# The first state products of a gated recurrence, made for one column instead of 512 and fed in as the gates' bias

## The reference, cut to what matters

```python
x = x + tanh(g_xattn[0]) * _L0_xattn_ref(_layernorm(x), ctx, ctx, ...)
x = x + tanh(g_ffn[0])   * _L0_ffn_ref(_layernorm(x), w_gate, w_up, w_down)
x = x + tanh(g_xattn[1]) * _L1_xattn_ref(_layernorm(x), ctx, ctx, ...)
x = x + tanh(g_ffn[1])   * _L1_ffn_ref(_layernorm(x), wf, uf, bf, ...)

# _L1_ffn_ref
c0 = jnp.broadcast_to(in_c, (batch, in_c.shape[0]))      # batch is 512 here
def step(c, xt):
    ft = sigmoid(xt @ wf.T + c @ uf.T + bf)
    it = sigmoid(xt @ wi.T + c @ ui.T + bi)
    gt = tanh(xt @ wc.T + c @ uc.T + bc)
    return ft * c + it * gt, None
c_final, _ = lax.scan(step, c0, x)                        # 4 steps
h = tanh(einsum('tbi,oi->tbo', x, wo) + c_final @ uo.T + bo)
```

## Time and profile before

| what | value |
|---|---|
| median of 3 runs | 343.23 us (343.20 to 343.27) |
| span of the profiled execution, first to last instruction | 341.2 us |
| what lies around the span (median less span) | 2.0 us |
| mean granted TensorE clock | 0.957 |
| PE busy | 279.0 us (82%) |
| DVE busy | 252.5 us (74%) |
| ACT busy | 192.6 us (56%) |
| POOL busy | 136.7 us (40%) |

### The profile page before, as it was taken

How to read it: one execution, slowest core, us unless ns; L and a number is a source line. 1 busy time by engine, 2 the same in 40 slices (tenths; PEclk the granted TensorE clock), 3 DMA queues, 4 the chain that set the end, 5 groups by cost and what they waited for, 6 DMA issues and landing times. The chain is left out here.

```text
span 341.2 us, 4468 instructions
## 1 busy us (share of the span) xinstructions
PE 279.0 (82%) x1424; PEld 160.7 (47%) x1424; DVE 252.5 (74%) x538; ACT 192.6 (56%) x303; POOL 136.7 (40%) x274
## 2 busy tenths in 40 slices
PE   0889899899989779985007888899998998999994
PEld 0558544455434345331005776664654654444462
DVE  5699875877996388889989977986596693441834
ACT  1673367556476746779589632446656446665232
POOL 6669893750050411870002059921386207131100
PEclk9999999999999999997556999999999999999998
DMA  7930100010000000000000002220001000000004
GB/s 204 336 146 3 69 32 10 27 73 10 1 8 3 0 0 2 1 0 0 1 0 0 2 0 92 94 100 2 10 25 76 8 0 10 1 0 3 0 1 123
DMA packets 9687, 12.55 MB, mean 37 GB/s; under 512 B 896, under 2 KB 5376, under 8 KB 9664
## 3 DMA queue, kind: packets, MB, share of 16 engines
q1 hardware_dynamic: 9232, 11.80, 9.7%
q10 hardware_dynamic: 432, 0.47, 0.7%
HBM read 4.27 MB, written 1.05 MB: 16 GB/s over the span
## 5 line engine op out<-in xcount | busy, mean ns | idle before, releaser
L1333 DVE TENSOR_REDUCE sb_nm<-ps_top 128x3 f32<-128x462 f32 (+2 forms) x168 | 96.0, 626 | 26.6 <-PE ps_top L953 13.9
L772 ACT ACTIVATE sb_pr<-ps_score 128x512 f32<-128x512 f32 (+1 forms) x148 | 82.3, 583 | 58.8 <-PE ps_score L985 49.2
L953 PE MATMUL ps_top<-sb_Kd,sb_Q 128*128 128x462 f32 (+3 forms) x240 | 69.7, 349 | 4.7 <-DVE sb_nm L1333 2.4
L985 PE MATMUL ps_score<-sb_Q,sb_Kd 128*128 128x512 f32 x119 | 54.4, 467 | 1.3 <-ACT sb_pr L772 1.0
L953 PEld LDWEIGHTS ps_top<-sb_Kd,sb_Q 128*128 128x128 f32 x240 | 42.6, 188 | 18.1 <-DVE sb_nm L1333 11.9
L626 POOL TENSOR_SCALAR sb_var<-sb_mv 128x4 f32<-128x4 f32 x16 | 4.7, 291 | 83.3 <-DVE sb_mv L1296 82.9
L985 PEld LDWEIGHTS ps_score<-sb_Q,sb_Kd 128*128 128x128 f32 x119 | 22.2, 188 | 31.6 <-ACT sb_pr L772 23.4
L1017 PE MATMUL ps_pv<-sb_pr,sb_V 128*32 128x512 f32 x256 | 34.1, 605 | 0.0
L620 POOL TENSOR_SCALAR_AFFINE_SELECT sb_pr<-sb_pr 128x512 f32<-128x512 f32 x16 | 10.6, 661 | 46.4 <-ACT sb_pr L772 46.4
L1353 DVE STREAM_TRANSPOSE sb_oq<-ps_pv 128x512 f32<-128x512 f32 x16 | 10.8, 700 | 12.4 <-PE ps_pv L1017 12.3
L643 POOL TENSOR_SCALAR sb_xn<-sb_xr,sb_nmean,sb_rstd 128x128 f32<-128x128 f32 x44 | 19.3, 453 | 1.2
(11 more groups left out here) (180 smaller groups left out, 556.5 us busy)
## 6 DMA issues: line engine op xcount, KB each, us to landing
sb_Q<-sb_qh SPq DMA_DIRECT2D x16, 256.0 KB, 2.3
sb_Q<-sb_ql SPq DMA_DIRECT2D x8, 256.0 KB, 3.3
sb_xr<-x SPq DMA_DIRECT2D x4, 256.0 KB, 7.7
out<-sb_xr SPq DMA_DIRECT2D x4, 256.0 KB, 2.5
sb_wsb<-w SPq DMA_DIRECT2D x1, 704.0 KB, 9.0
sb_wf<-wffn SPq DMA_DIRECT2D x1, 576.0 KB, 8.6
sb_wkr<-wkr SPq DMA_DIRECT2D x2, 256.0 KB, 7.1
sb_Q<-sb_nmT SPq DMA_DIRECT2D x16, 32.0 KB
```

Source lines behind the costliest of these rows:

```text
L772: act.activation(pr[:, k % PRING, q0:T], score_bank(B * layer + b, t)[:, q0:T], ACT.Exp, scale=SCALE).then_inc(exp_r, 1)
L953: ins = pe.matmul(cols[:, c0:c1, :], Q4[n % 3][:, g, P * qt:P * qt + P], Kd[n % 3][:, g, j:j + c1 - c0, 0:keys], start=True, stop=not mask ...
L985: ins = pe.matmul(ps[:, :], Kd[n % 3][:, g, j, 0:P], Q4[n % 3][:, g, :], start=True, stop=True, skip_group_check=True)
L1333: dve.tensor_reduce(nm[:, :, :].rearrange("p t h -> p (t h)")[:, f0:f0 + heads], top[k % MRING][:, 0:keys * heads].rearrange("p (h k) -> p ...
```

## The change

The initial state is equal in all columns, so its product with a recurrent weight is one column. The three state products of step 0 leave PE's slots 4, 6 and 8 of stage 3. In their place PE makes three products of one column each in the quantised block (`first_states`, into three columns of bank `top[1]`), DVE adds the gates' biases to them into a new tile `fcols` of 128 x 3 (`first_gates`, two instructions, ahead of the four `outer`), and ACT's first three gates take their bias from `fcols`. The input products of step 0 now start their PSUM banks themselves. Three waits on the new semaphore `fcol_r` and one on `fmul` come with it.

```diff
-           (4, "state0", "first"), (4, "step0", "first"), (6, "state1", "first"), (6, "step1", "first"),
-           (8, "state2", "first"), (8, "step2", "first"),
+           (4, "step0", "first"), (6, "step1", "first"), (8, "step2", "first"),
...
+        fcols = sb("fcols", [P, 3])
...
                 if b > 0:
                     act.wait_ge(c_r, b + 2)
-                bias = (hcols[:, BF:BF + 1], hcols[:, BI:BI + 1], cols_sb[:, BC:BC + 1])[k]
+                else:
+                    act.wait_ge(fcol_r, 2)
+                bias = ((hcols[:, BF:BF + 1], hcols[:, BI:BI + 1], cols_sb[:, BC:BC + 1])[k] if b > 0
+                        else fcols[:, k:k + 1])
...
+                if n == B and u == 0:
+                    pe.wait_ge(fcol_r, 2)
...
                     pe.wait_ge(c_r, b + 2)
-                    pe.wait_ge(top_red, units_before(2 * B))
-                if b > 0:
-                    pe.wait_ge(gt_r, 3 * b - 2 + k)
+                pe.wait_ge(gt_r, 3 * b - 2 + k)
...
+                if (b, k) == (0, 0):
+                    pe.wait_ge(top_red, units_before(2 * B))
...
-                ins = pe.matmul(top[k][:, :], weight((WF, WI, WC)[k]), pnT[:, b, :], start=(b == X_FIRST),
+                ins = pe.matmul(top[k][:, :], weight((WF, WI, WC)[k]), pnT[:, b, :], start=(b in (0, X_FIRST)),
...
+            def first_states():
+
+                pe.wait_ge(fev, 24)
+                pe.wait_ge(c_r, 2)
+                for k in range(3):
+                    ins = pe.matmul(top[1][:, k:k + 1], weight((UF, UI, UC)[k]), cst[:, 0:1], start=True, stop=True,
+                                    skip_group_check=True)
+                ins.then_inc(fmul, 1)
...
                     for k in range(2, 4):
                         global_top(k)
+                    first_states()
                     pe.wait_ge(fev, 24)
                     pe.wait_ge(o_r, 2)
                     keep_warm(6)
...
+                def first_gates():
+                    dve.wait_ge(fmul, 1)
+                    for k, bias in ((slice(0, 2), hcols[:, BF:BF + 2]), (slice(2, 3), cols_sb[:, BC:BC + 1])):
+                        dve.scalar_tensor_tensor(out=fcols[:, k], in0=top[1][:, k], scalar=1.0 if k.start else 0.5, in1=bias,
+                                                 op0=ALU.mult, op1=ALU.add).then_inc(fcol_r, 1)
...
                 factor(1, 1.0, sc[:, 3, 1:2], sc[:, 2, 1:2])
+                first_gates()
                 for c in range(B):
                     outer(c)
```

More of the change, by code:

```diff
@@ L369, in program @@
         gt_r, ct_r, c_r = sem("gt_r"), sem("ct_r"), sem("c_r")
+        fmul, fcol_r = sem("fmul"), sem("fcol_r")
         ymm, y_r = sem("ymm"), sem("y_r")
```

## The result

| | before | the change |
|---|---|---|
| median | 343.25 us (343.20 to 343.60, 4 runs) | 340.65 us (340.55 to 340.79, 4 runs) |
| span of the profiled execution | 341.2 us | 338.6 us |
| ratio | | 0.9925, 95% interval 0.991 to 0.994 |

The change is 2.6 us faster, 0.75%; the forecast was 340.75 in a range of 340.4 to 341.6.

The account below looks back on a forecast made before the run. The prediction took PE's queue in stage 3 of layer 1 as the bound: -2.58 us for the removed products plus 0.10 for the DVE pair gave -2.48, so 343.23 became 340.75 us, range 340.4 to 341.6.

Parts of the forecast that it names:

- PE's queue is the bound where the products stand, each worth 0.86: Stage 3 of layer 1: PE runs without waits, so removing three products of 0.86 us saves 2.58 us.
- The next bound doesn't eat it: Stage 3: ACT, score banks and DVE meet their waits after the removal, so the full 2.58 us remains.
- Behind tile 9 everything moves along: From exponential 9 on, ACT has no backlog; the bank exchange begins 2.58 us earlier and is as long as before.
- The rival in which the mask on POOL holds things up: ACT or POOL's mask holds the bank exchange, losing one product's worth: -1.72 + 0.10, so 341.6 us; chance 0.12.
- The columns end by 176.5 and cost nothing: Quantised block: three one-column products are ready by 176.5, while PE idles until 181.05, so they cost nothing on PE.
- The pair costs +0.10: Quantised block: DVE's two `first_gates` instructions ahead of `outer(0)` cost +0.10 us, between hidden and +0.48.
- The estimate worked out from the Trainium skill: Quantised block: at 120 cycles plus columns the DVE pair takes 0.25 us, is over at 177.32 and costs nothing.
- the 0.19 in front of `outer`: Quantised block: `outer(0)` begins 0.19 us after ACT's end; if set-up needing a free DVE, the pair costs +0.22.
- The clock: Rival: less busy PE drops to the lower clock, costing 7.9 us from 306.3 to 314.2, so 348.7 us; chance 0.02.

Follow-up runs that it names:

- five pairs: The change with the pair of DVE instructions made five times, each into its own three columns: 341.13 us, ratio 0.9940.
- the last three runs: On one chip: the change unedited, 341.01 us; without its one-column products and DVE pair, 341.04 us; with step 0's third input product in PE slot 11, 340.28 us.
- one product back, the first: The change with step 0's first state product made over 512 columns again, in slot 4: 341.52 us, ratio 0.9951.
- only the tile: The kernel before with nothing but the unused 3-column tile `fcols` added: 343.12 us, ratio 1.0001.
- columns where PE is full: The change with one more one-column product ahead of each of step 0's three input products: 341.60 us, ratio 0.9956.
- the third product back: The change with step 0's third state product made over 512 columns again, in slot 8: 341.31 us, ratio 0.9938.

## Why the prediction was right

- *PE's queue is the bound where the products stand, each worth 0.86.* Right, and shown: putting the third or the first back makes tile 9 later by 0.86 either way.
- *The next bound doesn't eat it.* Right for ACT and the banks: tile 9 moved by 2.58 against tile 4 (6.02 now, 301.17 - 292.57 = 8.60 before). DVE did become the later one at the new state, with 2.3 us of slack where I had reckoned 2.0.
- *Behind tile 9 everything moves along.* This step missed 0.16. I had taken it that the third mask on POOL moves along with the rest and stays as long. DVE's chain in front of the new state moved by 1.72 plus what `renew` allowed, so it no longer stands to the mask as before, and the two overlapped for 0.57 instead of 0.30. The run in which DVE waits for the mask gives the 0.16 back. The rival in which the mask on POOL holds things up was there, but priced at a whole product, 0.86.
- *The columns end by 176.5 and cost nothing.* Right; 1.28 us busy in place of the 1.8 reckoned, done at 175.48.
- *The pair costs +0.10.* Mis-sized, since it is 0.00 within 0.04. I had 0.34 for an instruction, from one of 128 columns and two partitions, and it is 0.16. The estimate worked out from the Trainium skill ("VectorE: DVE Perf Modes", section on the TRN2 errata), over by 177.32, came nearer: 0.22 from the first start to the last end, against 0.25. That is partly luck, since each of the two takes more than the estimate's 0.13 (0.16 and 0.15) and they overlap, where the estimate put one behind the other. And the 0.19 in front of `outer` isn't set-up of a free DVE, as the five pairs show.
- *The clock.* 1.00 in the stage, as before. What was taken away left PE as full as before, only for a shorter time. That no pause of PE brings the clock down is true of the stretch from 200 to 208 only: in the quantised block, where PE had waited 6.9 us for work, the granted clock was 0.50 in both kernels.

The two misses, 0.16 of loss not seen and 0.10 of cost that wasn't there, nearly cancel: the sum should have been 2.42 by the trace. That 340.75 came so near is in part luck. The medians differ by 2.60, and by 2.58 on the chip of the last three runs, but with intervals of 0.5 us to either side they can't tell 2.42 from 2.60.

The spans of the two traces differ by 2.60 as well. Behind step 1 they agree (341.2 - 306.45 = 34.75 before, 338.6 - 303.81 = 34.79 now), so some 0.2 lies ahead of tile 4. The changed instructions didn't bring it: at 173.40, before the first of them starts (174.20), the trace is already 0.24 ahead (DVE's reduction in front of the fourth maximum, 173.64 before), and from ACT's tiles to tile 4 both take 116.9. So does every other variant with a usable trace (116.8 to 116.9), but for the five pairs. What differs between executions is when ACT's tiles start: from 175.47 to 177.10 over twelve traces, 175.47 and 176.18 for the change itself. The four latest, 176.31 and up, are those in which PE's granted clock was 0.83 to 0.88 from 40 to 50 us (one product back, the first; five pairs; only the tile; columns where PE is full); the eight others had 1.00 there. What spreads those eight, and with it the 0.24, is not shown.

## What to carry to other kernels

An operand that is the same in every column can be multiplied once, where the engine idles, and come back as a bias that an instruction reads anyway; its worth is the full price of the products only where the chain runs through them without a wait. Slide the queue forward by what is removed and test each wait with its margin, and test the pairs of engines too that only hold each other up. A stretch that the busy rows show nearly full may be an exchange of two banks with room in it: the pitch of queued pieces tells, not the busy time, and moving a piece into such room is worth while only as long as what it feeds isn't late.

## What the runs showed of the hardware

The same POOL instruction, an affine select over 128 x 512 in f32, takes 0.64 us alone and 0.80 or 1.06 beside DVE's f32 instructions with two SBUF operands: 0.64 when DVE waited for it, 0.80 with an overlap of 0.30 us (303.76 against DVE's last instruction until 304.06), and 1.06 with 0.57. So it does not run slower for a share of the overlap: it loses all of it but 0.14 to 0.15. Put otherwise, it ends 0.49 to 0.50 behind the end of DVE's instruction, however long the two overlap (302.02 against 301.53 in the change, 304.56 against 304.06 before, 302.74 against 302.24 with the third product back), as if it stood still until DVE was done. DVE's instruction, which had begun first, kept its 0.69. Where DVE waited for the mask, its instruction met POOL's next one instead, one of two inputs on 128 x 4 (L629): overlap 0.45, and 1.33 us instead of 1.03, so again all but 0.15. Beside DVE's transposition from PSUM the mask isn't held: in the change the first mask (292.54) overlaps one that runs from 292.42 to 293.14, and takes 0.64.

A DVE instruction on one or two columns of PSUM takes 0.15 to 0.16 us, and ten in a row start 0.067 apart. A one-column f32 product takes 1.28/3 = 0.43 us of PE at the lower clock (granted 0.50, in the quantised block) and 0.23 in a full queue at the higher one (1.00).
